# Attention's weighted sums as two 64-row halves, issued beside scores and maxima, with the engine loops unrolled

## The chip, the cores and the metric

The kernel runs on one NeuronCore of a Trainium2 chip. The metric is device time in microseconds of one execution. Engines are TensorE (PE in the profile; its weight loads are PEld), VectorE (DVE), ScalarE (ACT), GpSimd (POOL) and SyncE (SP), which issues the DMAs. PSUM has eight banks of 128 x 512 float32.

## The reference

A transformer layer with attention and a feed-forward part side by side, float32, on 4 sequences of 2048 rows of 256:

```
xn  = layernorm(x)
qkv = xn @ W_qkv                               # 16 heads of 16
s   = q @ k.T + bias[bucket(key - query), head]   # 2048 x 2048 per head, 64 heads in all
a   = softmax(s) @ v
out = x + concat(a) @ W_out + gate(xn) * (gelu(xn @ w1 + b1) @ w2 + b2)
```

The bias depends only on the distance between key and query, and is constant for distances beyond 96 or so on either side.

## The kernel before, in words

There are three stages, each a block in which every engine has its own program. Stage one (0 to 590 us) makes the layer norm, q, k, v and the feed-forward part; it stores q and k to DRAM, split into a coarse and a fine part, so that a product of 48 stacked rows (three partial products of 16) gives a float32-like result in the fast format. Stage three (from 3454 us) does the output projection. Stage two, between them, is the attention and holds nearly all that the change touches.

**Stage two.** A head n has 16 key blocks kb of 128 keys; a block has four chunks c of 512 queries. Four heads make a group, and u = n mod 4 is the head's place in it. The stacks `q_st[u]`, `k_st[u]` of a head lie in partitions 0 to 48 for u = 0, 1 and in 64 to 112 for u = 2, 3. In each block TensorE does:

- `scores` (L960): keys by queries, 49 rows (48 and one with the negated row maximum) by 128 columns, 512 elements moving, into a ring of three PSUM banks (`RING`); it waits in `ring_free` until ScalarE has taken the tile three before it.
- `maxima` (L944): queries by keys of the head two ahead (`LEAD`), 48 rows, into two pairs of banks. This head's stacks lie in the other half of the partitions, so a score and a maximum product can run at the same time. VectorE reduces a pair of banks (L903) to a row maximum.
- `sums` of the block before, kb - 1 (L969): the four chunks' probabilities, all 128 keys as rows, by 32 columns of v (16 of v, one of ones, the rest zero). Chunk c's result goes to partitions 32c to 32c + 31 of bank 7, so the four products sit beside each other in the columns of the array. These operands are true float32, and each product runs as two passes, each with its own weight load.

ScalarE takes each score tile with an exponential into `prob` (L830), which holds two blocks; GpSimd multiplies the part near the diagonal by the bias (L874). Once per head TensorE also transposes the finished sums (L985, at block `TURN_RESULT` = 3) and the maxima (L956, at block 8), ScalarE copies them (L808, L814, L802), VectorE takes reciprocals (L916) and GpSimd normalises.

TensorE's order within a block is written out by hand in `head` (from L987): score 0, maximum 0, score 1, maximum 1, score 2, maximum 2, score 3, maximum 3, then four sums. Each engine works in its program's order. The first group (heads 0 to 3) and the last (60 to 63) are written out; the 14 groups between them are a `Fori` loop on each engine, which runs its body from one stretch of instructions with counters in registers. Stage one has `Fori` loops over the middle batches on SP, POOL, DVE and ACT (not on PE), stage three on its engines. SP brings the next head's stacks and bias once per head (L142, L768).

Of the kernel before, what the change touches and what calls it, by code (L numbers as in the profile page):

```python
# [42 lines left out]
LEAD = 2  # L43

# [47 lines left out]


def near_at(kb, c):

    found = [i for i, part in enumerate(near_parts(kb)) if part[0] // CH == c]
    return NEAR_UP_TO[kb] + found[0] + 1 if found else 0


def sum_order(kb):  # L100

    return sorted(range(CPB), key=lambda c: (near_at(kb, c) > 0, c))
# [25 lines left out]
def transformer_layer(nc, x, w_qkv, w_out, rel_emb, router_w, w1, b1, w2, b2, hot, out):  # L128
# [16 lines left out]
    with ctx:  # L145
# [21 lines left out]
        with c1:  # L167
# [98 lines left out]
            def _(sp):  # L266
# [59 lines left out]
                with sp.Fori(1, B) as b:  # L326
                    batch(b)
# [11 lines left out]
            def _(pool):  # L339
# [27 lines left out]
                with pool.Fori(1, B) as b:  # L367
                    batch(b)

            @block.vector  # L370
            def _(dve):
# [145 lines left out]
                with dve.Fori(1, B - 1) as b:  # L517
                    for c in range(CPB):
                        chunk(b, c, early=True)
# [4 lines left out]
            def _(act):  # L524
# [53 lines left out]
                with act.Fori(1, B - 1) as b:  # L578
                    for c in range(CPB):
                        chunk(b, c)  # L580
# [118 lines left out]
        with c2:  # L699
# [7 lines left out]
            prob = sb("prob", [P, 2, S], c=c2)  # L707
# [30 lines left out]
            TURN_RESULT, TURN_SHIFT = 3, 8  # L738
# [16 lines left out]
            def summed(n, kb, c):  # L755

                return CPB * (KB * n + kb) + sum_order(kb).index(c) + 1
# [4 lines left out]
            def _(sp):  # L762
# [30 lines left out]
                with sp.Fori(1, GROUPS - 1) as g:  # L793
                    group(g)
# [3 lines left out]
            def _(act):  # L798
# [5 lines left out]
                def collect(n):  # L804

                    wait(act, pv_done, CPB * KB * (n + 1))
                    wait(act, o_turned, n)
                    nc.scalar.activation(o_sb[:], ps[:, SUM_BANK], ACT.Copy).then_inc(o_copied, 1)  # L808
# [8 lines left out]
                def head(n, u, first=False, last=False):  # L817
                    for kb in range(KB):
                        if kb == 1 and not first:
                            collect(n - 1)  # L820
                        if kb == TURN_RESULT and not first:
                            collect_turned(n - 1)
                        if kb == TURN_SHIFT and not last:
                            shift(n + 1, (u + 1) % GROUP)
                        for c in range(CPB):
                            i = CPB * (KB * n + kb) + c
                            wait(act, score_ready, i + 1)

                            wait(act, pv_done, summed(n, kb - 2, c) if kb > 1 else summed(n - 1, KB + kb - 2, c))
                            nc.scalar.activation(prob[:, kb % 2, CH * c:CH * (c + 1)], ps[:, tile_at(kb, c) % RING], ACT.Exp).then_inc(drained, 1)  # L830
# [4 lines left out]
                with act.Fori(1, GROUPS - 1) as g:  # L835
                    for u in range(GROUP):
                        head(GROUP * g + u, u)
# [6 lines left out]
            def _(pool):  # L844
                def build(n, u, turn):
                    wait(pool, pv_done, CPB * KB * (n - 1))
# [15 lines left out]
                def head(g, u, first=False, last=False):  # L862
                    n = GROUP * g + u
                    for kb in range(KB):
# [6 lines left out]
                        for q0, q1, side, c0 in near_parts(kb):  # L871

                            wait(pool, drained, drained_at(n, tile_at(kb, q0 // CH)))
                            nc.gpsimd.tensor_tensor(prob[:, kb % 2, q0:q1], prob[:, kb % 2, q0:q1], near[u][:, side, c0:c0 + q1 - q0],  # L874
# [10 lines left out]
                with pool.Fori(1, GROUPS - 1) as g:  # L885
                    for u in range(GROUP):
                        head(g, u)
# [7 lines left out]
            def _(dve):  # L895
# [35 lines left out]
                with dve.Fori(1, GROUPS - 1) as g:  # L931
                    for u in range(GROUP):
                        head(GROUP * g + u, u)
# [5 lines left out]
            def _(pe):  # L939
# [32 lines left out]
                def sums(n, u, kb):  # L972

                    if kb == 0:

                        wait(pe, v_built, n + 1)
                        wait(pe, o_copied, n)
                    for c in sum_order(kb):
                        values(n, u, kb, c)
# [39 lines left out]
                with pe.Fori(1, GROUPS - 1) as g:  # L1019
# [4 lines left out]
                sums(NH - 1, NH - 1, KB - 1)  # L1024
# [7 lines left out]
        with c3:  # L1032
# [28 lines left out]
            def _(sp):  # L1061
# [19 lines left out]
                with sp.Fori(1, B - 1) as b:  # L1081
# [6 lines left out]
            def _(act):  # L1088
# [26 lines left out]
                with act.Fori(1, B - 1) as b:  # L1115
# [4 lines left out]
            def _(dve):  # L1120
# [22 lines left out]
                with dve.Fori(1, B - 1) as b:  # L1143
# [4 lines left out]
            def _(pe):  # L1148
# [30 lines left out]
                with pe.Fori(1, B - 1) as b:  # L1179
# [26 lines left out]
```

## Time and profile before

| | |
|---|---|
| median of 3 runs (lowest, highest) | 3522.74 us (3516.03, 3544.99) |
| profiled execution, its own time | 3528.89 us |
| its span, first to last instruction | 3527.1 us |
| mean granted TensorE clock | 0.971 |
| PE busy | 3293.2 us (93%), weight loads 1586.0 us |
| DVE, ACT, POOL busy | 2767.9 (78%), 2480.1 (70%), 1201.7 us (34%) |

Busy time counts an engine as working while at least one of its instructions runs, so two products at once count once, and TensorE's ends are modelled. A high share does not say that the array is full. Start times in the timeline say more: the distance from one start to the next is what an instruction really costs its successor. The granted clock is in shares of 2.4 GHz.

### The profile page before, as it was taken

How to read it: one execution, taken by the hardware profiler on the slowest of the kernel's cores; microseconds unless marked ns; L12 is line 12 of the kernel's file. 1: busy time of each engine (PE TensorE's matmuls, PEld its weight loads, DVE VectorE, ACT ScalarE, POOL GpSimd, SP SyncE). 2: the span in 40 equal slices, each digit the busy share in tenths (PEclk: the TensorE clock that was granted, in tenths of full speed). 3: DMA queues.
4: the chain of work that ended last, by engine and by line, in shares of the span. 5: the costliest groups of instructions: out<-in, count | busy, mean ns of one | idle time of the engine just before them, and what ended most of it. 6: DMA issues, size and time to landing. Idle time of an engine off the chain costs nothing. (4 is left out here: it accounts for less than half of the span.)

```text
span 3527.1 us, 71020 instructions
## 1 busy us (share of the span) xinstructions
PE 3293.2 (93%) x20426; PEld 1586.0 (45%) x20426; DVE 2767.9 (78%) x3046; ACT 2480.1 (70%) x4875; POOL 1201.7 (34%) x1644
## 2 busy tenths in 40 slices
PE   8899996799999999999999999999999999999998
PEld 7788885333333333333333333333333333333337
DVE  4477753688888888888888888888888888888814
ACT  4443433688878787878787878787878787878875
POOL 1121121333333333333333333333333333334330
PEclk9999998899999999999999999999999999999999
DMA  7422323100000000000000000000000000000006
GB/s 179 120 79 82 98 88 95 34 28 28 28 28 27 28 27 28 27 28 27 28 27 28 27 28 27 28 28 28 28 28 28 28 28 28 28 28 28 14 1 194
DMA packets 80559, 157.57 MB, mean 45 GB/s; under 512 B 8088, under 2 KB 48728, under 8 KB 73864
## 3 DMA queue, kind: packets, MB, share of 16 engines
q1 hardware_dynamic: 80200, 152.90, 14.8%
q8 instruction: 211, 3.46, 0.4%
q14 instruction: 148, 1.21, 0.1%
HBM read 101.92 MB, written 56.16 MB: 45 GB/s over the span
## 5 line engine op out<-in xcount | busy, mean ns | idle before, releaser
L903 DVE TENSOR_REDUCE max_half<-ps 128x1 f32<-128x1024 f32 x1984 | 2337.1, 1220 | 417.6 <-PE ps L944 414.2
L830 ACT ACTIVATE prob<-ps 128x512 f32<-128x512 f32 x4096 | 2116.8, 603 | 566.1 <-PE ps L960 564.5
L960 PE MATMUL ps<-q_st,k_st 49*128 49x512 f32 x4096 | 1536.1, 454 | 193.2 <-ACT prob L830 48.2
L944 PE MATMUL ps<-k_st,q_st 48*128 48x512 f32 x3968 | 1589.3, 474 | 0.0
L874 POOL TENSOR_TENSOR prob<-prob,near 128x224 f32<-128x224 f32 (+2 forms) x1408 | 963.1, 690 | 1751.7 <-ACT prob L830 1732.8
L960 PEld LDWEIGHTS ps<-q_st,k_st 49*128 49x128 f32 x4096 | 692.4, 188 | 1398.6 <-ACT prob L830 1166.6
L969 PE MATMUL ps<-prob,vx 128*32 128x512 f32 x4096 | 959.6, 618 | 0.0
L969 PE MATMUL ps<-prob,vr 128*32 128x512 f32 x4096 | 958.5, 616 | 0.0
L944 PEld LDWEIGHTS ps<-k_st,q_st 48*128 48x128 f32 x3968 | 669.5, 188 | 55.5 <-DVE max_half L903 1.0
L606 PE MATMUL ps<-xnt,w_parts 128*128 128x512 f32 x1152 | 277.9, 401 | 16.8 <-DMA k_early<-qk_parts 10.9
L606 PEld LDWEIGHTS ps<-xnt,w_parts 128*128 128x128 f32 x1152 | 218.9, 192 | 70.3 <-DMA k_early<-qk_parts 11.1
L547 ACT ACTIVATE parts<-ps 128x512 fp32r<-128x512 f32 x64 | 38.3, 598 | 272.7 <-PE ps L606 234.0
L969 PEld LDWEIGHTS ps<-prob,vr 128*32 128x32 f32 x4096 | 133.7, 108 | 175.5 <-ACT prob L830 145.1
L671 PE MATMUL ps<-w_parts,hid 128*128 128x256 f32 x1536 | 196.7, 284 | 0.0
L671 PEld LDWEIGHTS ps<-w_parts,hid 128*128 128x128 f32 x1536 | 184.3, 189 | 11.7 <-issue 11.7
L969 PEld LDWEIGHTS ps<-prob,vx 128*32 128x32 f32 x4096 | 133.3, 108 | 81.4 <-ACT prob L830 51.1
L358 POOL TENSOR_TENSOR top_exp<-euler,top_less 128x32 f32<-128x32 f32 x16 | 86.8, 5428 | 159.8 <-DVE top_less L411 159.8
L352 POOL TENSOR_TENSOR rstd<-var_eps,power 128x4 f32<-128x4 f32 x17 | 23.1, 1356 | 309.7 <-DVE var_eps L386 309.7
L555 ACT ACTIVATE hid_raw<-ps,b_sb 128x512 f32<-128x512 f32 x128 | 88.1, 689 | 42.3 <-PE ps L606 32.5
L473 DVE TENSOR_TENSOR hid<-hid_raw,hid 128x512 fp32r<-128x512 f32 x128 | 85.4, 688 | 19.4 <-ACT hid L562 16.6
L456 DVE TENSOR_TENSOR parts<-ps,parts 128x512 fp32r<-128x512 f32 x64 | 44.2, 691 | 71.8 <-ACT parts L547 69.7
L446 DVE TENSOR_REDUCE max_early<-ps 128x1024 f32 x64 | 78.4, 1225 | 22.1 <-PE ps L615 19.0
(70 smaller groups left out, 1060.7 us busy)
## 6 DMA issues: line engine op xcount, KB each, us to landing
qk_parts<-parts SPq DMA_DIRECT2D x64, 512.0 KB, 4.7
near<-bias_near SPq DMA_DIRECT2D x64, 352.0 KB, 13.1
q_st<-qk_parts SPq DMA_DIRECT2D x64, 256.0 KB
k_st<-qk_parts SPq DMA_DIRECT2D x64, 256.0 KB
x_sb<-in_L_attn_hidden_states SPq DMA_DIRECT2D x18, 512.0 KB, 6.0
base_rows<-x_sb SPq DMA_DIRECT2D x16, 512.0 KB, 2.9
q_st<-qk_parts SPq DMA_DIRECT2D x64, 128.0 KB
k_st<-qk_parts SPq DMA_DIRECT2D x64, 128.0 KB
```

The source lines that it names most:

```text
L358: nc.gpsimd.tensor_tensor(top_exp[:], euler[:], top_less[:], ALU.pow).then_inc(exp_done, 1)
L446: nc.vector.tensor_reduce(max_early[:, :, bass.ds(i, 1), j], ps[:, 0:2].unsqueeze(2), AX.X, ALU.max).then_inc(max_done, 1)
L473: nc.vector.tensor_tensor(hid[:, 1, f], hid_raw[:, f % RAWS], hid[:, 0, f].bitcast(F32), ALU.subtract).then_inc(hid_low, 1)
L555: nc.scalar.activation(hid_raw[:, f % RAWS], ps[:, F1_BANKS[f % 4]], ACT.Gelu_apprx_tanh, bias=b1_sb[:, f:f + 1]) \
L606: last = nc.tensor.matmul(to, stationary(a, k), moving(b, k), start=k == 0 and (a, b) == PASSES[0], stop=k == blocks - 1 and (a, b) == PAS ...
L671: last = nc.tensor.matmul(ps[:, F2_BANKS[t % 2], E * (t // 2):E * (t // 2 + 1)], hid[:, a, f, P * t:P * (t + 1)], weight(W_2, b_, f), star ...
L830: nc.scalar.activation(prob[:, kb % 2, CH * c:CH * (c + 1)], ps[:, tile_at(kb, c) % RING], ACT.Exp).then_inc(drained, 1)
L874: nc.gpsimd.tensor_tensor(prob[:, kb % 2, q0:q1], prob[:, kb % 2, q0:q1], near[u][:, side, c0:c0 + q1 - q0], ALU.mult).then_inc(near_done, 1)
L903: nc.vector.reduce_max(max_half[:, par % 2, i, half:half + 1], ps[:, MAX_BANK + 2 * half:MAX_BANK + 2 + 2 * half].rearrange("p a n -> p (a ...
L944: mm = nc.tensor.matmul(ps[:, MAX_BANK + c], q_st[u][0:ROWS, P * i:P * (i + 1)], k_st[u][0:ROWS, CH * c:CH * (c + 1)], start=True, stop=True)
L960: nc.tensor.matmul(ps[:, tile_at(kb, c) % RING], k_st[u][:, P * kb:P * (kb + 1)], q_st[u][:, CH * c:CH * (c + 1)], start=True, stop=True). ...
L969: nc.tensor.matmul(ps[32 * c:32 * (c + 1), SUM_BANK], v[:, u % 2, kb], prob[:, kb % 2, CH * c:CH * (c + 1)], start=kb == 0, stop=kb == KB ...
```

## The change

In stage two:

- `sums` issues 64 keys (rows) at a time: half 0 or 1 of `vx`/`vr` and of `prob`. Four products of one half, then at another place in the block four of the other half, accumulating into the same partitions of bank 7. So there are eight products (sixteen passes) per block where there were four (eight passes).
- The half whose rows are not those of the current head's stacks, `1 - u // 2`, is issued between score 0 and scores 1 to 3; the other half, `u // 2`, between maximum 1 and maxima 2 and 3. Scores and maxima are no longer interleaved: score 0, sums, scores 1 to 3, maxima 0 and 1, sums, maxima 2 and 3.
- Sums run two blocks behind (`LAG` = 2) and `prob` holds four blocks (`PROBS` = 4). `TURN_RESULT` becomes 4, since the last sums of a head end a block later.
- What the sums need is waited for ahead of score 0 (`sums_ready`), among it that the previous block's sums are complete; before maximum 1 TensorE waits until its own first half is complete (`first_half_done`).
- `near_at` and `sum_order` go, and the chunks are taken in order.

In all stages each `Fori` loop becomes a Python loop, so every iteration has instructions of its own.

```diff
 LEAD = 2
+PROBS = 4
+LAG = 2
...
-            prob = sb("prob", [P, 2, S], c=c2)
+            prob = sb("prob", [P, PROBS, S], c=c2)
...
-            TURN_RESULT, TURN_SHIFT = 3, 8
+            TURN_RESULT, TURN_SHIFT = 4, 8
...
-                return CPB * (KB * n + kb) + sum_order(kb).index(c) + 1
+                return 2 * CPB * (KB * n + kb) + CPB + c + 1
...
-                        if kb == 1 and not first:
+                        if kb == LAG and not first:
                             collect(n - 1)
...
-                            wait(act, pv_done, summed(n, kb - 2, c) if kb > 1 else summed(n - 1, KB + kb - 2, c))
+                            wait(act, pv_done, summed(n, kb - PROBS, c) if kb >= PROBS else summed(n - 1, KB + kb - PROBS, c))
...
-                def values(n, u, kb, c):
-                    if near_at(kb, c):
-                        wait(pe, near_done, NEAR_UP_TO[KB] * n + near_at(kb, c))
-                    else:
-                        wait(pe, drained, drained_at(n, tile_at(kb, c)))
-                    v = vr if c < left_chunks(kb) else vx
-                    nc.tensor.matmul(ps[32 * c:32 * (c + 1), SUM_BANK], v[:, u % 2, kb], prob[:, kb % 2, CH * c:CH * (c + 1)],
-                                     start=kb == 0, stop=kb == KB - 1).then_inc(pv_done, 1)
...
+                def sums_ready(n, kb):
+
+                    wait(pe, near_done, NEAR_UP_TO[KB] * n + NEAR_UP_TO[kb + 1])
+                    wait(pe, drained, drained_at(n, tile_at(kb, CPB - 1)))
+                    wait(pe, pv_done, 2 * CPB * (KB * n + kb))
+
+                def sums_begin(n):
+
+                    pe.wait_ge(v_built, 1)
+                    wait(pe, o_copied, n)
+
+                def first_half_done(n, kb):
+
+                    wait(pe, pv_done, 2 * CPB * (KB * n + kb) + CPB)
+
+                def sums(n, u, kb, half, turn):
+
+                    for c in range(CPB):
+                        v = vr if c < left_chunks(kb) else vx
+                        rows = slice(HALF * half, HALF * (half + 1))
+                        nc.tensor.matmul(ps[32 * c:32 * (c + 1), SUM_BANK], v[rows, u % 2, kb], prob[rows, kb % PROBS, CH * c:CH * (c + 1)],
+                                         start=kb == 0 and turn == 0, stop=kb == KB - 1 and turn == 1).then_inc(pv_done, 1)
...
-                        for c in range(CPB):
+                        there = kb >= LAG or not first
+                        vn, vu, vb = (n, u, kb - LAG) if kb >= LAG else (n - 1, u + 1, KB + kb - LAG)
+
+                        if there:
+                            sums_ready(vn, vb)
+                            if vb == 0:
+                                wait(pe, v_built, vn + 1)
+                        scores(n, u, kb, 0)
+                        if there:
+                            if vb == 0:
+                                sums_begin(vn)
+                            sums(vn, vu, vb, 1 - u // 2, 0)
+                        for c in range(1, CPB):
                             scores(n, u, kb, c)
-                            if left >= LEAD:
-                                maxima(m, mu, kb, c)
-                        if kb > 0:
-                            sums(n, u, kb - 1)
-                        elif not first:
-                            sums(n - 1, u + 1, KB - 1)
+                        if left >= LEAD:
+                            maxima(m, mu, kb, 0)
+                        if there:
+                            first_half_done(vn, vb)
+                        if left >= LEAD:
+                            maxima(m, mu, kb, 1)
+                        if there:
+                            sums(vn, vu, vb, u // 2, 1)
+                        if left >= LEAD:
+                            maxima(m, mu, kb, 2)
+                            maxima(m, mu, kb, 3)
...
-                with pe.Fori(1, GROUPS - 1) as g:
+                for g in range(1, GROUPS - 1):
                     for u in range(GROUP):
                         head(g, u)
```

The same replacement of `Fori` stands on every engine in stages one, two and three.

## Rows read from the trace of the kernel before

**Rows 1.** The page: busy time by engine, and the span in 40 slices.

```profile
PE 3293.2 (93%) x20426; PEld 1586.0 (45%) x20426; DVE 2767.9 (78%) x3046; ACT 2480.1 (70%) x4875; POOL 1201.7 (34%) x1644
...
PE   8899996799999999999999999999999999999998
```

**Rows 2.** Timeline, one block: start us, us, engine line op out<-in xcount [idle before<-releaser]

```profile
1500.96 0.49 PE L960 MATMUL ps<-q_st,k_st 49*128 49x512 f32 x1
...
1501.29 0.39 PE L960 MATMUL ps<-q_st,k_st 49*128 49x512 f32 x1
...
1501.53 0.39 PE L960 MATMUL ps<-q_st,k_st 49*128 49x512 f32 x1
...
1502.14 0.49 PE L960 MATMUL ps<-q_st,k_st 49*128 49x512 f32 x1
...
1502.14 0.50 PE L944 MATMUL ps<-k_st,q_st 48*128 48x512 f32 x1
1502.57 0.12 PEld L969 LDWEIGHTS ps<-prob,vr 128*32 128x32 f32 x3 [0.24 <-ACT prob L830]
1502.57 0.63 PE L969 MATMUL ps<-prob,vr 128*32 128x512 f32 x3
...
1502.60 0.12 PEld L969 LDWEIGHTS ps<-prob,vr 128*32 128x32 f32 x3
...
1503.02 0.60 PE L969 MATMUL ps<-prob,vr 128*32 128x512 f32 x3
...
1503.57 0.18 PEld L960 LDWEIGHTS ps<-q_st,k_st 49*128 49x128 f32 x1 [0.84 <-ACT prob L830]
1503.57 0.50 PE L960 MATMUL ps<-q_st,k_st 49*128 49x512 f32 x1
```

**Rows 3.** Timeline, the same block: the first exponentials and reductions, and the next.

```profile
1501.49 2.06 ACT L830 ACTIVATE prob<-ps 128x512 f32<-128x512 f32 x4 [0.54 <-PE ps L960]
...
1501.76 2.36 DVE L903 TENSOR_REDUCE max_half<-ps 128x1 f32<-128x1024 f32 x2 [0.25 <-PE ps L944]
...
1504.10 2.06 ACT L830 ACTIVATE prob<-ps 128x512 f32<-128x512 f32 x4 [0.55 <-PE ps L960]
```

**Rows 4.** Timeline in stage one: 128-row products, then two of 48 rows, then back.

```profile
202.60 0.19 PEld L615 LDWEIGHTS ps<-k_early,q_early 48*128 48x128 f32 x2 [0.37 <-issue]
202.60 0.50 PE L615 MATMUL ps<-k_early,q_early 48*128 48x512 f32 x2
...
203.03 0.53 PEld L606 LDWEIGHTS ps<-xnt,w_parts 128*128 128x128 f32 x3 [0.25 <-issue]
```

**Rows 5.** Timeline: the sums, the four transposes of L985, the next score.

```profile
1427.61 1.07 PE L969 MATMUL ps<-prob,vx 128*32 128x512 f32 x8
1428.60 0.42 PEld L985 LDWEIGHTS ps<-ident,o_sb 128*128 128x128 f32 x4 [0.84 <-ACT prob L830]
1428.61 0.66 PE L985 MATMUL ps<-ident,o_sb 128*128 128x128 f32 x4
1429.19 0.18 PEld L960 LDWEIGHTS ps<-q_st,k_st 49*128 49x128 f32 x1 [0.17 <-issue]
```

**Rows 6.** L808, once per head: heads 2 to 7, 10 to 61, 61 to 64.

```profile
L808 ACT ACTIVATE o_sb<-ps x6: 597/598/599, 723.6 to 937.6; 128x512 f32<-128x512 f32 x6
...
L808 ACT ACTIVATE o_sb<-ps x52: 597/598/600, 1071.8 to 3326.5; 128x512 f32<-128x512 f32 x52
...
L808 ACT ACTIVATE o_sb<-ps x4: 597/598/599, 3326.5 to 3453.4; 128x512 f32<-128x512 f32 x4
```

**Rows 7.** L830 over the whole run: duration min/median/max, first and last start.

```profile
L830 ACT ACTIVATE prob<-ps x4096: 589/603/630, 633.8 to 3451.0; 128x512 f32<-128x512 f32 x196
```

**Rows 8.** TensorE where a loop iteration begins, and two stretches of it by window.

```profile
1509.25 0.78 PE L960 MATMUL ps<-q_st,k_st 49*128 49x512 f32 x1 [3.01 <-issue]
...
1507.00:1514.00 7.00, 4.75 (x18) 2.05 (x20) 2.36 (x2) 2.51 (x5) 0.67 (x1) 0.54 0.42 113
1514.00:1521.00 7.00, 7.00 (x32) 2.13 (x28) 4.49 (x4) 4.47 (x9) 1.87 (x2) 0.50 0.13 54
```

More of the change, by code:

```diff
@@ L91 @@
 NEAR_UP_TO = [sum(len(near_parts(i)) for i in range(kb)) for kb in range(KB + 1)]
[L94 to L102, printed above, removed]
 def bucket_line():
@@ L325, in _ @@
                     load_stacks(sp, h, q_early[HALF * h:HALF * h + ROWS], k_early[HALF * h:HALF * h + ROWS], early_in)
-                with sp.Fori(1, B) as b:
+                for b in range(1, B):
                     batch(b)
@@ L366, in _ @@
                 batch(0)
-                with pool.Fori(1, B) as b:
+                for b in range(1, B):
                     batch(b)
@@ L516, in _ @@
                     chunk(0, c)
-                with dve.Fori(1, B - 1) as b:
+                for b in range(1, B - 1):
                     for c in range(CPB):
@@ L577, in _ @@
                     chunk(0, c)
-                with act.Fori(1, B - 1) as b:
+                for b in range(1, B - 1):
                     for c in range(CPB):
@@ L804, in collect @@
                 def collect(n):
-                    wait(act, pv_done, CPB * KB * (n + 1))
+                    wait(act, pv_done, 2 * CPB * KB * (n + 1))
                     wait(act, o_turned, n)
@@ L834, in _ @@
                     head(u, u, first=u == 0)
-                with act.Fori(1, GROUPS - 1) as g:
+                for g in range(1, GROUPS - 1):
                     for u in range(GROUP):
@@ L845, in build @@
                 def build(n, u, turn):
-                    wait(pool, pv_done, CPB * KB * (n - 1))
+                    wait(pool, pv_done, 2 * CPB * KB * (n - 1))
                     pool.wait_ge(v_ones_set, 2)
@@ L884, in _ @@
                     head(0, u, first=u == 0)
-                with pool.Fori(1, GROUPS - 1) as g:
+                for g in range(1, GROUPS - 1):
                     for u in range(GROUP):
@@ L930, in _ @@
                     head(u, u, first=u == 0)
-                with dve.Fori(1, GROUPS - 1) as g:
+                for g in range(1, GROUPS - 1):
                     for u in range(GROUP):
@@ L1018, in _ @@
                     head(0, u, first=u == 0)
-                with pe.Fori(1, GROUPS - 1) as g:
+                for g in range(1, GROUPS - 1):
                     for u in range(GROUP):
@@ L1023, in _ @@
                     head(GROUPS - 1, u, left=GROUP - 1 - u)
-                sums(NH - 1, NH - 1, KB - 1)
+                for kb in range(KB - LAG, KB):
+                    sums_ready(NH - 1, kb)
+                    sums(NH - 1, NH - 1, kb, 0, 0)
+                    first_half_done(NH - 1, kb)
+                    sums(NH - 1, NH - 1, kb, 1, 1)
                 ring_free(NH - 1, RING_TILES - 1 + RING)
@@ L1080, in _ @@
                 batch(0)
-                with sp.Fori(1, B - 1) as b:
+                for b in range(1, B - 1):
                     batch(b)
@@ L1114, in _ @@
                 batch(0)
-                with act.Fori(1, B - 1) as b:
+                for b in range(1, B - 1):
                     batch(b)
@@ L1142, in _ @@
                 batch(0)
-                with dve.Fori(1, B - 1) as b:
+                for b in range(1, B - 1):
                     batch(b)
@@ L1178, in _ @@
                 batch(0)
-                with pe.Fori(1, B - 1) as b:
+                for b in range(1, B - 1):
                     batch(b)
```

11 lines of the change are left out of this document (2 added, 9 removed).

## The prediction, made blind

> **What bounds the kernel now.** I read the page's busy shares first [rows 1]: TensorE 93%, VectorE 78%, ScalarE 70%. The slices show that stage two is uniform, so one block of it is worth reading start by start. The first exponential starts at 633.8 and the last at 3451.0 [rows 7]: this stage takes 2818 of the 3527 us.
>
> In a block [rows 2] the first score starts at 1500.96, the next block's at 1503.57: 2.61 us. Scores start 0.33 and 0.24 apart, and each has its maximum product running beside it (the last one's starts within 0.01 us of it). The fourth waits for the first exponential to free a ring bank (1502.14). Then come the sums: first pass 0.43 after the score, second pass 0.45 later, next score 0.55 after that. So 1.43 us from the last score to the next block's first one. That piece is the bound: ScalarE works 2.06 us in four exponentials and then idles 0.54 us waiting for a score, VectorE works 2.36 us in two reductions and idles 0.25 us [rows 3]. The bound is a circle: exponential 0, score 3, sums, next score 0, next exponential 0.
>
> Sixteen blocks of 2.61 are 41.8 us. Heads are 42.8 us apart where no iteration boundary lies between (five intervals from 723.6 to 937.6 [rows 6]), so the transposes and copies of a head cost 1.0 us. With one boundary in four heads they are 44.2 us apart (51 intervals from 1071.8 to 3326.5).
>
> **The loops.** The difference, 1.4 us a head, belongs to the iteration boundaries. At one of them TensorE idles 3.01 us with no releaser but issue, and then runs at a granted clock of 0.54 and 0.50, that is mostly 1.2 GHz, for some 14 us [rows 8]. With 64 heads at 42.8 the stage would be 2739 us, 2818 - 2739 = 79 us less. The written-out first group and the step from it into the loop show no longer heads, so I count the whole 79 us as gain where TensorE stays as busy. In stages one and three I count nothing: PE has no loop in stage one, and the other engines are ahead of it or wait for it; at the worst, fetching more code costs a few us there.
>
> **The sums.** What is removed: four products of 128 rows (two passes) from the end of the block. What is added: eight products of 64 rows (four sets of passes), as a pass of a half streams the same 512 elements for each chunk. The passes cost 0.45 us per set [rows 2] whatever the number of rows, by my estimate: nothing in the rows shows a 64-row float32 pass, and between 0.24 (a 49-row score) and 0.45 (the same format) I take the one of the same format. So the array is only paid back if a half's passes run at the same time as scores or maxima in the other half of the rows.
>
> No row shows products of different shape at once; it must be bounded. One end: full overlap. The other: none. What lies nearest is what TensorE does when the shape changes. Score to sums takes 0.43 us, where score to score after the same unprepared weights takes 0.33; second pass to score takes 0.55, where pass to pass takes 0.45 [rows 2]. So a change of shape adds 0.10 us, and the new weights are not loaded before, though the weights of pass two are loaded at 1502.60 while pass one streams through the very same rows. The same at a change of rows alone, 128x128 to 48x128 and back (0.43 from 202.60 to 203.03, weights loaded only then) [rows 4], and from 32 columns to 128 over the same 128 rows: the transposes' weights start at 1428.60, with the loader idle for 0.84 us before [rows 5]. Three kinds of change, and each waits until what is in the array has passed. If the array were kept free row by row, I would expect at least the weights to be pulled ahead. I take the end without overlap.
>
> The Trainium skill says as much, and beyond the rows, since it exempts no disjoint rows: its page "TensorEngine Tiling (Array Packing)", section "Tiling Modes", states that changing the tiling mode, not just the tile, drains TensorE, and lists 64x128 and 64x32 as two modes.
>
> **The new block without overlap,** from max 2 on, by start-to-start distances from [rows 2]: max 2 to max 3 0.33 (weights unprepared); score 0 beside max 3 (other rows, same shape) 0; score to first pass 0.33 (0.43 less the 0.10 for unprepared weights); to second pass 0.45; to score 1 0.55; to score 2 0.33; to score 3 0.24; max 0 beside it 0; max 1 0.24; to sums 0.33; second pass 0.45; to max 2 0.55. Sum 3.80 us. Scores 1 to 3 and the maxima lose each other as company, which is part of this price. No other engine is late at 3.80: ScalarE needs 2.06, VectorE 2.36 [rows 3]. The ring wait of score 3 (for the exponential of score 0, ready 1.9 us earlier) is covered. The wait for the first half before maximum 1 has its sums 1.4 us behind it, the one before score 0 has the second half's last pass started 0.88 us before and 0.60 long; both are covered, the second by 0.3 us only. Behind either stand all later products, so ScalarE and VectorE would feel it. GpSimd has two blocks now instead of one. SP's loads per head are unchanged, with 62 us to come in instead of 43.
>
> The turns of a head cost 1.0 now. They get shape changes on both sides where maxima and score would have met: 1.4. A head is 16 x 3.80 + 1.4 = 62.2 us; 62 of them 3856. The last two heads have no maxima: 0.43 + 0.45 + 0.55 + 0.33 + 0.24 + 0.33 + 0.45 + 0.55 = 3.33 a block, 54.7 a head, 109. The two blocks of sums left at the end and the two missing at the start cancel. Stage two: 3965, against 2818, +1147 (the loops' gain is in it, as no boundary is counted). Against the profiled execution's 3528.9 us: 4676. The median of the runs is 6 us below it, so **4670 us**. Its own range: 4300 if the 0.10 per change vanishes (four a block, 410 us), 4900 if the waits on its own passes or the missing look-ahead of weights bite by 0.2 us a block. The clock stays at 1.0 as TensorE doesn't idle.
>
> **Rival A, faster: the halves do overlap.** Products start in order, but a half's passes share the time of scores or maxima in the other rows. Block: score 0 and pass one 0, pass two 0.45, scores 1 to 3 behind it in 0.7, max 1 at 1.15, sums again, 0.45, maxima 2 and 3, next score at 2.1. Then TensorE is no longer the bound, and VectorE is: two reductions in 2.36 us, some of it overlapping the next, so 2.3. A head 16 x 2.3 + 0.8 = 37.6, 62 of them 2331; two heads at ScalarE's 2.06, 67; 2398. 2818 - 2398 = 420: about 3100 us, 3300 if in-order waits cost 0.2 us a block. I name 3140. For it: scores and maxima do overlap, 0.01 apart, in disjoint rows [rows 2], and weights for the other half are loaded meanwhile. Against it: both have the same shape, and each of the three changes of shape in the rows waits. The Trainium skill's page "TensorE: Matmul & The Clock Gate", section "Part 3: Packing small matmuls", speaks for this rival: it says that weight loads are pulled ahead wherever row groups differ, and packed products overlap. No row here shows that across shapes. Chance 0.26.
>
> **Rival B, the sums gain nothing:** overlap as in A, but TensorE stands before maximum 1 until its first half is complete, and before score 0 for the second. Each exposes about a pass's 0.60 duration less what is issued meanwhile, 0.2 to 0.3 us, on the 2.1; with ring waits the block is back at 2.6. Then only the loops pay: 3529 - 79 = 3450, or with 2.68 a block 3520. Chance 0.08, half of it within 1%.
>
> **Rival C, slower for another reason: the code supply.** Written out, TensorE's program is fetched once and for all, 16 passes a block and no reuse. If the 3.01 us of [rows 8] came per stretch of code and not per jump, each head would pay the boundary's 5.6 us (four heads at 1.4): 64 x 5.6 = 358, on rival A's 3140 3500 or so, on B's 3450 3810. Against: heads 2 to 7 run at 42.8, half of them through code met for the first time [rows 6]. Chance 0.02.
>
> **How the numbers follow.** No overlap 0.64, A 0.26, B 0.08, C 0.02. About 1% (35 us) is what a measurement tells from no change. Faster: A and half of B, 0.30. Within 1%: 0.04. Slower: 0.66. The likeliest case's range of 4300 to 4900 holds only some 0.6 by itself, and the faster case must be in: 3130 to 4850, wide because the one unknown, whether two shapes share the array, has two far ends.
>
> **What would show it.** Right: a block of about 3.8 us in the timeline; L969 never starting within 0.05 us of a following L960 in other rows but 0.55 after; ScalarE idle 1.7 us a block behind L960; VectorE idle similarly behind L944. Wrong: scores starting less than 0.3 us after a sums pass, and VectorE over 90% busy in stage two. The loops' part is right if no 3 us gap with issue as releaser stands at the group boundaries and the clock stays at 1.0 through stage two. If the changes of shape cost nothing but the overlap is absent, the block is near 3.4 us.

## The result, and the profile after

The changed kernel takes **7490.38 us** (median of 4 runs, 7489.6 to 7490.89) against 3519.39 for the kernel before: ratio 2.123, 95% interval 2.112 to 2.134. The forecast was slower, 4670 us, in a range up to 4850. The time lies far outside.

The page of the profile after, lines that answer to [rows 1], and the slices of the granted clock:

```profile
PE 7392.5 (99%) x28618; PEld 2572.6 (34%) x28618; DVE 2861.2 (38%) x3046; ACT 2598.0 (35%) x4875; POOL 1193.6 (16%) x1644
...
PEclk9995555555555555555555555555555555555556
```

TensorE is busy 99% of the span, and from the start of the attention stage to its end it is granted half of its clock, 1.2 GHz. One block of the changed kernel, by start times (columns as in [rows 2]):

```profile
4999.38 1.06 PE L974 MATMUL ps<-prob,vr 64*32 64x512 f32 x1
...
5000.23 1.06 PE L974 MATMUL ps<-prob,vr 64*32 64x512 f32 x1
...
5001.24 0.79 PE L951 MATMUL ps<-q_st,k_st 49*128 49x512 f32 x1
5001.25 0.79 PE L935 MATMUL ps<-k_st,q_st 48*128 48x512 f32 x1
5001.83 0.62 PE L951 MATMUL ps<-q_st,k_st 49*128 49x512 f32 x1
5001.85 0.62 PE L935 MATMUL ps<-k_st,q_st 48*128 48x512 f32 x1
5002.07 1.57 ACT L821 ACTIVATE prob<-ps 128x512 f32<-128x512 f32 x3 [1.98 <-PE ps L951]
5002.26 0.62 PE L951 MATMUL ps<-q_st,k_st 49*128 49x512 f32 x1
...
5002.81 1.06 PE L974 MATMUL ps<-prob,vr 64*32 64x512 f32 x1
```

The reader is to see two things. The pass that starts at 5000.23 is followed by score 1 only 1.01 us later: nothing of another shape starts while a pass runs. And each distance is nearly doubled: pass to pass 0.85 (0.45 in [rows 2]), score to score 0.59 (0.33). A block takes 6.44 us (median) where it took 2.61. ScalarE idles 1.98 us for score 1. The loss of some 3970 us has two parts, then: a longer block and a lower clock. The experiments take them apart.

### The profile page after: what moved, and what is told of

Its sections match the earlier page's. It is cut to its first block and busy times, and to the rows that moved or that the text cites. A ratio compares the mean times of both kernels' runs of the same rounds, so it can differ in the third digit from the quotient of the medians.

```text
span 7487.8 us, 74824 instructions
## 1 busy us (share of the span) xinstructions
PE 7392.5 (99%) x28618; PEld 2572.6 (34%) x28618; DVE 2861.2 (38%) x3046; ACT 2598.0 (35%) x4875; POOL 1193.6 (16%) x1644
## 5 line engine op out<-in xcount | busy, mean ns | idle before, releaser
L894 DVE TENSOR_REDUCE max_half<-ps 128x1 f32<-128x1024 f32 x1984 | 2429.5, 1225 | 4160.1 <-PE ps L935 4160.1
L821 ACT ACTIVATE prob<-ps 128x512 f32<-128x512 f32 x4096 | 2224.1, 598 | 4050.3 <-PE ps L951 4042.3
L974 PE MATMUL ps<-prob,vr 64*32 64x512 f32 x8192 | 3437.3, 1057 | 0.8 <-PE ps L974 0.5
L974 PE MATMUL ps<-prob,vx 64*32 64x512 f32 x8192 | 3437.2, 1057 | 0.0
L951 PE MATMUL ps<-q_st,k_st 49*128 49x512 f32 x4096 | 2463.5, 701 | 54.4 <-DMA k_st<-qk_parts 43.5
L935 PE MATMUL ps<-k_st,q_st 48*128 48x512 f32 x3968 | 2416.4, 708 | 0.0
L951 PEld LDWEIGHTS ps<-q_st,k_st 49*128 49x128 f32 x4096 | 1136.1, 306 | 1919.8 <-issue 1812.5
L935 PEld LDWEIGHTS ps<-k_st,q_st 48*128 48x128 f32 x3968 | 998.7, 296 | 1647.7 <-DVE max_half L894 1647.7
L974 PEld LDWEIGHTS ps<-prob,vr 64*32 64x32 f32 x8192 | 331.0, 135 | 996.7 <-issue 991.0
L974 PEld LDWEIGHTS ps<-prob,vx 64*32 64x32 f32 x8192 | 330.9, 135 | 143.9 <-issue 143.9
```

What stands on the lines that cost most here:

```text
L821: nc.scalar.activation(prob[:, kb % PROBS, CH * c:CH * (c + 1)], ps[:, tile_at(kb, c) % RING], ACT.Exp).then_inc(drained, 1)
L894: nc.vector.reduce_max(max_half[:, par % 2, i, half:half + 1], ps[:, MAX_BANK + 2 * half:MAX_BANK + 2 + 2 * half].rearrange("p a n -> p (a ...
L935: mm = nc.tensor.matmul(ps[:, MAX_BANK + c], q_st[u][0:ROWS, P * i:P * (i + 1)], k_st[u][0:ROWS, CH * c:CH * (c + 1)], start=True, stop=True)
L951: nc.tensor.matmul(ps[:, tile_at(kb, c) % RING], k_st[u][:, P * kb:P * (kb + 1)], q_st[u][:, CH * c:CH * (c + 1)], start=True, stop=True). ...
L974: nc.tensor.matmul(ps[32 * c:32 * (c + 1), SUM_BANK], v[rows, u % 2, kb], prob[rows, kb % PROBS, CH * c:CH * (c + 1)], start=kb == 0 and t ...
```

## Experiments: the parts of the change in the kernel

**E1 and E16, the loops only** (the kernel before; one kernel, run twice):

```diff
-                with pe.Fori(1, GROUPS - 1) as g:
+                for g in range(1, GROUPS - 1):
```

> The kernel before with only the loops written out; sums, their place and the two blocks of probabilities stay. If the loop part of the prediction holds (3 us without instructions and 14 us at 1.2 GHz at each of 14 boundaries), the stage of attention loses 79 us and the time is about 3440 us, with no gap of 3 us and a granted clock of 1.0 from 650 us on. Rival: writing out the code costs as much as it saves, by later code arriving late, or the clock falls for good as in the changed kernel: 3520 us, or far above 5000.

> The kernel of e1 again, to see how often its attention stage stays at 1.2 GHz. Theory: one run in four or so at 4610 us, the rest at 3450. Rival: that run was a single event, all at 3450.

Measured 3451.2 us, ratio 0.9795 (0.9769 to 0.9822), and again 3449.8, ratio 0.978 (0.973 to 0.984). The counterpart of [rows 8]:

```profile
645.00:3370.00 2725.00, 2607.24 (x16502) 1026.10 (x16498) 2350.66 (x2102) 2183.64 (x4267) 1081.31 (x1591) 1.00 0.09 27
```

The clock is 1.00 throughout, and 71 us are gained of the 79 predicted. The trace of the kernel before has 13 boundaries in the attention stage, not 14; TensorE idles 2.4 to 3.2 us at each, and the clock is then at 1.2 GHz for 3.4 to 13.7 us, so the 14 us of [rows 8] are the longest case. One of the ten executions, in E1, took 4612 us at a mean clock of 0.555; the other nine took 3447.6 to 3494.8. No profile of the long one was kept, but its mean clock is that of a stage at 1.2 GHz: a kernel with 128-row sums can stay there too.

**E2, both sets with all rows:**

```diff
-                        rows = slice(HALF * half, HALF * (half + 1))
+                        rows = slice(0, P)
```

> The changed kernel, its order, waits and number of products kept, but each of the two sets of sums takes all 128 rows. Everything is summed twice, numerator and denominator alike, so the quotient is unchanged. Theory: the clock was lost because the passes fill only half of the rows; with full rows the granted clock is near 1.0 and the block costs what the distances of the kernel before give in this order, about 3.6 us (max 0 and 1 run beside scores 1 and 2), so 4430 us. Rival: the clock was lost through the four changes of shape in a block or the way the stage starts; then this stays at 1.2 GHz and at 7490 us.

Measured 4608.1 us, mean clock 0.991, ratio 1.308 (1.305 to 1.312); blocks of 3.72 us. The same number of passes, in the same places, behind the same waits, and the clock is back: in the profile it rises to 2.4 GHz at 643.0 and stays there through the attention stage. This splits the loss: loops -71, no overlap and two more sets of passes +1157 (E2 less E1), clock +2882 (the change less E2).

**E12, the halves without the new order** (two 64-row sets at the block's end, scores and maxima in turn):

```diff
-                        scores(n, u, kb, 0)
+                        for c in range(CPB):
+                            scores(n, u, kb, c)
+                            if left >= LEAD:
+                                maxima(m, mu, kb, c)
...
                             sums(vn, vu, vb, 1 - u // 2, 0)
...
                             first_half_done(vn, vb)
...
                             sums(vn, vu, vb, u // 2, 1)
```

> The changed kernel with the order of before: scores and maxima in turn, then both halves of the sums one behind the other, the second after the wait for the first. No dense products ahead. Theory: halves alone, without being placed beside anything, cost two more passes (0.90) and a wait on the first half's own end (0.2 to 0.3), so 3.75 us a block at 2.4 GHz and 4620 us; whether the clock rises is open: pairs fill both halves for 1 us of it, the passes fill half for 1.8 us. If it stays at 1.2 GHz: 6.5 us a block and over 7300 us, and then it is the half-filled passes and not the separation of scores and maxima that keep it down.

Measured 7474.5 us, clock 0.543. So the halves keep the clock down without the new order too; the order makes a difference of 16 us. E15 below is the same order with one 128-row set, at a mean clock of 0.971.

**E3, one 128-row set, scores apart from maxima:**

```diff
-                        rows = slice(HALF * half, HALF * (half + 1))
+                        rows = slice(0, P)
...
-                            sums(vn, vu, vb, 1 - u // 2, 0)
...
-                            first_half_done(vn, vb)
...
-                            sums(vn, vu, vb, u // 2, 1)
+                            sums(vn, vu, vb, 1, 1)
```

> The changed kernel with one set of sums of 128 rows in a block, at the second of the two places, and the first set left away; so nothing of the work is missing, there are two changes of shape in a block instead of four, and the scores stay apart from the maxima. Theory (half-filled passes cost the clock, changes of shape cost 0.10 each and no overlap): clock 1.0, block 2.6 to 2.8 us, 3470 to 3650 us. If separating scores and maxima is what lowers the clock or costs the time: 1.2 GHz, above 4500 us.

Measured 5947.6 us, clock 0.553, 4.95 us a block. A miss: full rows are not enough. Part of a block, from maximum 2 to the sums, and below it the same eight products at the same 1.2 GHz without waits (E8, stretch 10, before its clock rises):

```profile
2004.65 0.79 PE L935 MATMUL ps<-k_st,q_st 48*128 48x512 f32 x1
...
2006.59 0.29 PEld L951 LDWEIGHTS ps<-q_st,k_st 49*128 49x128 f32 x1 [0.61 <-ACT prob L821]
2006.60 1.22 PE L935 MATMUL ps<-k_st,q_st 48*128 48x512 f32 x2
2007.74 1.07 PE L970 MATMUL ps<-prob,vr 128*32 128x512 f32 x3
```

```profile
964.72 2.08 PE L178 MATMUL ps<-mr,wr 64*128 64x512 f32 x8
```

In the kernel the eight products take 3.09 us to the sums, alone 2.01 (the sums follow at 966.73). The fourth score waits for ScalarE's first exponential to free its bank, and maxima 0 and 1, which stand behind it, start with it or later (from 2006.60); alone, each of the four maxima starts beside a score. VectorE is not waited for: maximum 2 starts 1.01 us after the second pass, as score 1 does in the changed kernel.

**E15, the distance of two blocks alone** (128-row set at the end, pairs in turn):

> The change without its halves and without its new order: sums two blocks behind from four blocks of probabilities, 128 rows in one set at the end of the block, scores and maxima in turn, loops written out. Theory: the distance does nothing, since sums never waited for ScalarE or GpSimd: 2.61 us a block, 3450 us, clock near 0.99. Rival: the distance or the gathered waits ahead of score 0 cost time or clock: 3550 us and more.

Measured 3864.7 us, ratio 1.093 (1.087 to 1.099), blocks of 3.02 us. A miss too, with a plain cause:

```profile
2005.89 0.60 PE L970 MATMUL ps<-prob,vx 128*32 128x512 f32 x3
2006.87 0.46 PE L951 MATMUL ps<-q_st,k_st 49*128 49x512 f32 x1 [0.37 <-PE ps L970]
```

`sums_ready` waits ahead of score 0 until the previous sums are complete. When they are TensorE's last work, the score follows 0.98 us after the second pass instead of 0.55: the wait costs 0.43. In the changed kernel maximum 2 and 3 lie between, and it is covered.

**E7, the set between pair 2 and pair 3**, loops written out, dense start as in E6:

> Warm start, loops written out, sums two blocks behind with 128 rows in one set as in the kernel before, scores and maxima again in turn, and the set issued between the pair of chunk 2 and the pair of chunk 3, where score 3 has to wait for the first exponential anyway. Theory (two changes of shape in a block, the circle of exponential 0, score 3, sums broken): a block of 2.45 to 2.5 us instead of 2.61, 3290 to 3330 us. Rival: score 2 of the next block now waits for exponential 3 and the block stays at 2.6, 3440 us.

Measured 4037.5 us, ratio 1.143 (1.137 to 1.149), clock 0.995. In the block from 2002.28 to 2005.55, from maximum 2 on:

```profile
2003.70 0.50 PE L936 MATMUL ps<-k_st,q_st 48*128 48x512 f32 x1 [0.17 <-DVE max_half L895]
2004.12 1.06 PE L971 MATMUL ps<-prob,vx 128*32 128x512 f32 x8
2005.12 0.50 PE L952 MATMUL ps<-q_st,k_st 49*128 49x512 f32 x1
```

I had followed ScalarE only. Maximum 2 waits for VectorE's second pair of banks, the sums stand behind it, and maximum 3 behind the sums: one circle opened, another closed, 3.27 us.

## Experiments: shapes and the clock, TensorE alone

These kernels compute nothing of the layer; they issue stretches of products on the layer's input with no waits inside a stretch. Each was executed once.

**E4, each stretch after dense 128x128 products:**

> TensorE alone, no waits, ten stretches of products in a row, each after some 27 us of dense 128x128 products; the layer isn't computed. Order: 1 pairs of fast 64x128 products, one in each half of the rows; 2 one half only; 3 fast 64x128 in one half, four float32 64x32 in the other; 4 fast 64x128 and float32 64x128; 5 float32 64x128 and four float32 64x32; 6 four float32 64x32 in one half, four in the other; 7 four float32 128x32; 8 four float32 64x32 in one half only; 9 the changed kernel's block; 10 the same with 128-row sums. Theory (shapes bar overlap): a round of stretch 3 costs 1.5 us (0.33+0.45+0.55 and more), of stretch 5 2.4 us or so, stretch 4 only 0.9 (the wide pair overlaps whatever the format) and stretch 6 0.9. Rival (formats bar it, not shapes): stretch 3 and 4 are both serial, stretch 5 overlaps at 0.9. Clock: theory says it falls from 1.0 in stretches 2, 8, 3 and 9, where half of the rows stand empty, and stays in 1, 7, 6 and 10.

Stretches 2, 3, 4, 5, 6, 8 and 9 (from:to, length, TensorE busy and count, weight loads, three idle engines' columns, clock, DMA share, GB/s):

```profile
120.00:176.00 56.00, 56.00 (x248) 45.46 (x247) 0.00 (x0) 0.00 (x0) 1.00 0.00 1
212.00:354.00 142.00, 142.00 (x499) 26.32 (x495) 0.00 (x0) 0.00 (x0) 0.50 0.00 0
384.00:435.00 51.00, 51.00 (x181) 22.47 (x180) 0.00 (x0) 0.00 (x0) 1.00 0.00 0
463.00:564.00 101.00, 101.00 (x493) 22.28 (x492) 0.00 (x0) 0.00 (x0) 1.00 0.00 1
593.00:644.00 51.00, 51.00 (x953) 18.27 (x960) 0.00 (x0) 0.00 (x0) 1.00 0.01 2
760.00:819.00 59.00, 59.00 (x552) 17.40 (x548) 0.00 (x0) 0.00 (x0) 1.00 0.00 1
848.00:911.00 63.00, 63.00 (x430) 19.42 (x423) 0.00 (x0) 0.00 (x0) 1.00 0.00 1
```

*Shapes.* Stretch 4, fast and float32 products of the same 64x128 shape in different rows: 60 rounds in 51 us, 0.85 each, as long as two float32 passes take in stretch 8; the fast one adds nothing. Stretch 6, eight 64x32 products in both halves: again 0.85 a round, as for four (stretch 8: 70 rounds in 60 us). Stretch 5, both float32, 64x128 in one half and 64x32 in the other: 50 rounds in 102 us, 2.03, that is 0.85 + 0.85 and both changes. So products in the two halves overlap when they have one shape, and don't when they have two, with the formats alike or not. The rival, that the formats bar the overlap, is refuted. *Clock.* Only stretch 3 fell to 1.2 GHz; 2, 8 and 9 held 2.4 GHz with half of the rows empty. My theory of the clock was wrong here: the changed block alone ran at 2.4 GHz, 3.54 us.

**E8, each stretch after 17 us of rest:**

> TensorE alone again, ten stretches, but each after some 17 us in which it has nothing to do, so that it begins at 1.2 GHz; the layer isn't computed. Order: 1 pairs of fast 64x128; 2 one half of them only; 3 four float32 128x32; 4 four float32 64x32; 5 four float32 64x32 in either half; 6 fast and float32 64x128 side by side; 7 the changed kernel's block; 8 the same with 128-row sums; 9 the block of the kernel before (four pairs, 128-row sums); 10 scores and maxima apart, one 128-row set. Theory (it takes more to get the clock up than to keep it, and half-filled rows don't do it): 1, 3, 5, 6 and 8 rise to 2.4 GHz soon after their start, 9 too but perhaps late, and 2, 4, 7 and 10 stay at 1.2 GHz. Rival: all rise, and what kept the clock down in the kernels was their waits on other engines.

Stretches 1 to 10, each read from behind its first microseconds:

```profile
30.00:82.00 52.00, 52.00 (x462) 47.57 (x460) 0.00 (x0) 0.00 (x0) 1.00 0.01 1
100.00:207.00 107.00, 107.00 (x251) 82.63 (x251) 0.00 (x0) 0.00 (x0) 0.50 0.00 0
231.00:287.00 56.00, 56.00 (x528) 15.48 (x516) 0.00 (x0) 0.00 (x0) 1.00 0.00 1
305.00:424.00 119.00, 119.00 (x560) 26.77 (x552) 0.00 (x0) 0.00 (x0) 0.50 0.00 1
449.00:505.00 56.00, 56.00 (x1048) 16.92 (x1032) 0.00 (x0) 0.00 (x0) 1.00 0.01 2
523.00:643.00 120.00, 120.00 (x211) 46.66 (x209) 0.00 (x0) 0.00 (x0) 0.50 0.00 0
660.00:777.00 117.00, 116.90 (x433) 31.58 (x433) 0.05 (x1) 0.00 (x0) 0.50 0.00 0
801.00:861.00 60.00, 60.00 (x408) 18.64 (x400) 0.00 (x0) 0.00 (x0) 1.00 0.00 1
883.00:943.00 60.00, 60.00 (x458) 23.39 (x456) 0.00 (x0) 0.00 (x0) 1.00 0.00 1
968.00:1028.00 60.00, 60.00 (x451) 23.48 (x449) 0.00 (x0) 0.00 (x0) 1.00 0.00 1
```

TensorE is busy all the time in each, and yet 2, 4, 6 and 7 stay at 1.2 GHz to their end, while the others rise. Beside E4 this is the finding: the half-filled stretches 2 and 8 of E4 and the changed block hold 2.4 GHz when they find it, but from 1.2 GHz they did not reach it in 107 to 119 us. The other stretches rose within 3 to 6 us. The state at a stage's start matters as much as its block. Stretch 6 stays low although it uses both halves; its fast product runs beside only one of the two float32 passes of a round. Against my list only 6 (predicted to rise) and 10 (to stay) differ.

**E13, 48 rows in scores and maxima, as in the kernel:**

> TensorE alone, eight stretches; the layer isn't computed. Four each begin after dense products (2.4 GHz): 1 the changed kernel's block with scores and maxima of 64 rows; 2 the same with 48 rows; 3 one 128-row set, scores and maxima apart, 48 rows; 4 the order of before, 48 rows. Then the same four, each after 17 us of rest (1.2 GHz). Theory (the emptier the rows, the lower): 1 holds 2.4 GHz as in e4, 2 falls, 3 and 4 hold; from rest 1 and 2 stay low, 4 rises, 3 may do either. Rival (the waits in the kernel did it): 2 behaves like 1 in both.

After dense products all four stretches held 2.4 GHz (355 us in one piece, the dense products between them included). From rest both changed blocks stayed at 1.2 GHz for some 116 us, while the 128-row orders rose after 6 and 8 us. So it makes no difference whether scores and maxima fill 48 or 64 rows.

**E18, long stretches:**

> TensorE alone, four long stretches of 64 changed blocks (scores and maxima of 48 rows), 226 us each at 2.4 GHz, each after dense products; the layer isn't computed. 1 as in e13; 2 with a head's transposes every 16 blocks, four of 128 columns at block 4 and one of 16 at block 8; 3 as 1 with zeros as the sums' moving operand; 4 as 1 with exp(x - 9), small numbers as probabilities are. If the turns end it: 1 holds 2.4 GHz throughout, 2 falls within its first 16 blocks. If the data do: 3 or 4 fall and 1 doesn't. If it is only time: all fall after 60 us or so. If all hold, it is the waits on other engines in the kernel.

Windows of stretch 1, of stretch 2 before and after its fall, of stretches 3 and 4; then the last transpose before the fall:

```profile
36.00:262.00 226.00, 226.00 (x1536) 69.77 (x1534) 0.00 (x0) 0.00 (x0) 0.00 (x0) 1.00 0.00 1
290.00:430.00 140.00, 140.00 (x937) 44.17 (x935) 0.00 (x0) 0.00 (x0) 0.00 (x0) 1.00 0.00 1
440.00:592.00 152.00, 152.00 (x565) 41.03 (x557) 0.00 (x0) 0.00 (x0) 0.00 (x0) 0.50 0.00 0
624.00:849.00 225.00, 225.00 (x1533) 69.43 (x1525) 0.00 (x0) 0.00 (x0) 0.00 (x0) 1.00 0.00 1
878.00:1104.00 226.00, 226.00 (x1535) 69.72 (x1527) 0.00 (x0) 0.00 (x0) 0.00 (x0) 1.00 0.00 1
```

```profile
436.45 0.28 PE L207 MATMUL ps<-ident,m 128*16 128x128 f32 x1
```

Stretches 1, 3 and 4 held 2.4 GHz for 226 us, so neither time nor data (zeros, small numbers) end it. Stretch 2 differs in nothing but a head's turns (its transposes), and it fell at 438.4, 2 us behind the transpose of block 8 of its third head. So the turns can end it. They did not at their first time, as I had expected: two heads passed before.

## Experiments: raising the clock in the kernel

**E5, E9 and E14, dense products before the stage** (42, 50 and 66 of them; in E14 the scores' operands are also filled with zeros to 64 rows):

```diff
                 turn_shift(0, 0)
+                moving = v_all[:].rearrange("p n k d -> p (n k d)")
+                for i in range(WARM):
+                    nc.tensor.matmul(ps[:, SUM_BANK], ident[:], moving[:, 0:CH], start=True, stop=True)
                 pe.wait_ge(stacks_in[0], 16 * STACK_LOADS)
```

> The changed kernel, and while TensorE waits 44 us for the first head's stacks at the start of the attention stage it runs 42 dense float32 128x128 products into the sums' bank, which nobody reads. Theory now: the changed block keeps the clock that it starts with; alone it ran at 3.54 us a block with the clock at 1.0 when dense products stood before it, while in the kernel the stage starts at 1.2 GHz after the idle time and stays there. Then this runs at a granted clock near 1.0 in the stage, 3.55 us a block, and takes 4550 to 4650 us. Rival: the block with its waits cannot hold the clock whatever stands before it; then it falls back within the stage and the time stays near 7490 us.

> As e5, with 50 dense products instead of 42. In e5 they ended 5.0 us before the stacks came, the clock fell to 1.2 GHz in that gap and the stage ran there as before. With 50 no gap is left and the changed block starts at 2.4 GHz. Theory (it keeps the clock it starts with): the blocks cost what they cost with full rows in e2, 3.72 us, and the time is 4600 us. Rival: the block, with the waits it has in the kernel, can't hold the clock; it falls within the stage and the time is 7490 us or, if it falls late, between.

> The changed kernel with 66 dense products ahead of the stage and the scores' operands filled up to 64 rows with zeros (49 before), maxima as they are. The zeros add nothing to the result and no time to a product. If the rows decide, and a quarter of them in half of the products is enough, the stage stays at 2.4 GHz: 3.72 us a block, 4610 us. If it isn't enough or the waits decide: 7500 us.

Measured 7490.3, 7489.0 and 7519.4 us: no gain. In E5 the clock fell in a gap of 5.0 us before the stacks. In E9 there was no gap; windows of its dense products, its first blocks and the rest:

```profile
600.00:632.00 32.00, 32.00 (x76) 14.17 (x75) 0.00 (x0) 0.00 (x0) 1.04 (x1) 1.00 0.28 85
632.00:639.00 7.00, 6.38 (x30) 2.69 (x29) 4.21 (x4) 4.62 (x9) 1.93 (x3) 1.00 0.13 53
641.00:7400.00 6759.00, 6748.70 (x24690) 2025.40 (x24682) 2445.98 (x2105) 2308.07 (x4270) 1074.85 (x1593) 0.50 0.04 11
```

It fell at 639.2, 6 us into the stage and 1.3 us after the start of the first sums (637.9); the two blocks ahead of them have no sums at all. E14 (one execution) fell likewise, so it says nothing on the rows.

**E17, the dense products behind those two blocks** (30, before the first sums):

> The changed kernel with 30 dense float32 128x128 products after the second block of the first head, that is right before the first block with sums. In e9 and e14 the dense products stood before the stage, and the clock fell in the first two blocks, which have scores and maxima but no sums; the changed block never got to run at 2.4 GHz. Theory (the changed block keeps the clock it finds, as it did alone in e4 and e13): from there on 2.4 GHz for the stage, 3.72 us a block as in e2, 4620 to 4640 us. Rival (its waits or the turns in a head bring it down): it falls within a head or a few, and the time is 7300 to 7520 us, or between if it falls late.

Measured 7501.6 us, but now six blocks ran at 2.4 GHz. One of them, from 676.75 to 680.47, and the place where the clock falls:

```profile
676.75 0.50 PE L952 MATMUL ps<-q_st,k_st 49*128 49x512 f32 x1
676.76 0.49 PE L936 MATMUL ps<-k_st,q_st 48*128 48x512 f32 x1
677.09 0.39 PE L952 MATMUL ps<-q_st,k_st 49*128 49x512 f32 x1
677.10 0.39 PE L936 MATMUL ps<-k_st,q_st 48*128 48x512 f32 x1
677.32 0.39 PE L952 MATMUL ps<-q_st,k_st 49*128 49x512 f32 x1
677.65 0.61 PE L975 MATMUL ps<-prob,vr 64*32 64x512 f32 x1
...
678.64 0.73 PE L936 MATMUL ps<-k_st,q_st 48*128 48x512 f32 x2
679.08 0.47 PE L952 MATMUL ps<-q_st,k_st 49*128 49x512 f32 x1
679.48 0.61 PE L975 MATMUL ps<-prob,vr 64*32 64x512 f32 x1
...
680.47 0.50 PE L952 MATMUL ps<-q_st,k_st 49*128 49x512 f32 x1
...
690.42 0.28 PE L948 MATMUL ps<-ident,max_neg 128*16 128x128 f32 x1
...
692.11 0.79 PE L952 MATMUL ps<-q_st,k_st 49*128 49x512 f32 x1
```

The block takes 3.72 us, as in E2, now with the 64-row halves themselves. The clock fell at 691.9, 1.5 us behind the head's transpose of block 8 at 690.42, the same place in the head as in E18. The rival was right. That the turn is the cause here as well is argued from the place; the waits on other engines are in this run too.

**E10, E3 with dense products and no gap:**

> As e3 (one 128-row set of sums, scores apart from maxima), started at 2.4 GHz by 50 dense products. e3 took 4.95 us a block at 1.2 GHz, though the same order of products without waits rises to 2.4 GHz by itself. Theory: it keeps the clock it starts with, a block of about 3.05 us (VectorE's pair of banks is waited for before maximum 2) and 3900 us in all. Rival: its waits make it fall, 5940 us.

Measured 5945.9 us, clock 0.557; the clock fell at 638.4, in the first blocks, as in E9. So the run does not tell whether its block would hold the clock.

**E6 and E11, the kernel of E1 with 42 and 50 dense products:**

> The kernel before with its loops written out and the same dense products in the 44 us of waiting. Theory: one of the four runs of the loops-only kernel took 4612 us at a mean clock of 0.555 as it never left 1.2 GHz after the start of the stage; with the dense products every run is at a clock of 0.99 and takes 3440 to 3450 us. Rival: the low run had another cause, and one such run can come again.

> As e6 with 50 dense products: the kernel before, loops written out, and no gap before the stage. The clock is at 1.0 from the first block, which saves the 14 us that e6 still spent at 1.2 GHz at less than double speed, some 7 us: 3443 us, every run alike. If dense products held up the first scores, as they end 1 us later than the stacks come, at most 3 us of that is lost.

E6: 3450.1 us, ratio 0.977 (0.973 to 0.981), six executions from 3448.1 to 3451.4. That none stayed low proves little beside one in ten without the products. E11: 3470.8, ratio 0.983 (0.980 to 0.986), a miss of 28 us: four of its six executions took 3470.7 to 3471.0, two 3452.2 and 3452.6. The profile, of one of the four, has no low clock in the first blocks, but 61 us of it from 3332.9, in the last heads, which have no maxima. E6, E1 and E16 are the same by measurement and the fastest found, some 2% faster than the kernel before.

## Why the prediction was wrong

- **What bounds the kernel before**: right as far as tested. E15 made the piece from the sums to the next score 0.43 us longer, and the block grew by 0.41. E7 broke this circle, but its order closed another one through VectorE's pairs of banks.
- **The loops**, -79 us: right in kind, measured -71 (E1), 5.5 us at each of 13 boundaries.
- **"I take the end without overlap"**: right, and the reason too: the shape decides, not the format or the rows (E4). Rival A and with it B fell. The Trainium skill's page "TensorEngine Tiling (Array Packing)", section "Tiling Modes", had it, and the runs agree (2.03 us a round against 0.85).
- **The new block, 3.80 us at 2.4 GHz**: right in size, 3.72 measured (E17). Two terms were off in opposite ways: maxima 0 and 1 run beside scores 1 and 2, not behind score 3 (-0.24); from maximum 2 by score 0 to the sums it is 0.84, not 0.66 (+0.18). That they cancel is luck. E2, with as many passes and 2.4 GHz in the stage, took 4608 us against the 4670 of the forecast.
- **"The clock stays at 1.0 as TensorE doesn't idle."** This step failed, and with it the time: 2882 of the 3970 us. It took TensorE's busy share for what the clock follows. The kernel before had shown the contrary in [rows 8], a window of 7 us at 0.50 of the clock in which TensorE was busy 7.00 of 7.00 us, and I read it as the tail of the 3 us gap only. The stage starts at 1.2 GHz in both kernels, after 44 us of waiting for the stacks. The block before brought the clock up at 643.9, some 11 us into the stage; the changed one never did, though TensorE was busy 6690 of 6700 us (700 to 7400) at 0.50. The Trainium skill's page "TensorE: Matmul & The Clock Gate", section "Part 1: The HAM clock gate", says that low is the default and activity releases it; a busy share of 99% here did not, so "busy" in the profile is not that activity.
- The chances were on the right side (slower 0.66), and not by luck: without overlap the kernel is slower at 2.4 GHz too (E2). But no case in the list held a low clock in the stage, so the range ended 2640 us short.

**Shown:** half-filled sums keep the stage at 1.2 GHz (the change against E2, E12 against E15; E8, stretch 7 against 8); the changed block alone holds 2.4 GHz and does not reach it from 1.2 (E4, E8, E13, E18); a head's turns can end it (E18). **Only argued:** that a turn ended it in E17, at the same place in the head. **Open:** what exactly the clock follows. 128-row sums don't always bring it up: one execution of E1 stayed low, and one 128-row set with scores apart from maxima stays low in the kernel (E3) though it rises alone within 8 us (E8, stretch 10; E13). Between two turns E3 has up to 59 us (12 blocks), so the turns alone hardly explain it. What differs besides is the wait for ScalarE ahead of score 3, by which fewer products run side by side (3.09 us against 2.01); no run tests it.

## What to carry to other kernels

Price a product that fills fewer rows not only by its start-to-start time but by what it leaves of the granted clock, and look at the clock a stage starts with: read the clock of every stretch where TensorE is busy without a gap, as those stretches show whether the work raises it. Products in disjoint rows overlapped here if they had one shape; before placing one beside another, make their shapes equal or count a full wait on each side. Writing out loops was worth the gap and the slow tail at each boundary between iterations, here 5.5 us a boundary.

## What the runs showed of the hardware that was not expected

- TensorE starts products in another order than the program's: in the rows of the change maximum 0 (5001.25) starts before scores 2 and 3 (5001.83 and 5002.26), which stand ahead of it. The Trainium skill's page "TensorE: Matmul & The Clock Gate", section "Part 3: Packing small matmuls", says that products start in order; here, in different rows, they don't.
- The clock has memory: fast 64x128 products in one half ran 56 us at 2.4 GHz after dense work (E4, stretch 2) and 107 us at 1.2 GHz after rest (E8, stretch 2).
- A wait of TensorE for its own last product costs 0.43 us when nothing stands between (E15).
